# Attention heads by halves: units of half a head, v in two column halves, short runs for o, sums scaled on GpSimd

## The chip, the cores and the metric

One core of a Trainium2 chip runs the whole program. The metric is the device time of one execution in microseconds; the kernel before takes 5920.14 us (median of 3 runs, 5917.19 to 5921.82).

## The reference

The program is four blocks in a row on a tensor of 4 x 96 x 64 x 64: a gated state-space block, a block with window-wise sedenion weights and an MLP, a local attention block with an MLP, and a selective scan. The change lies in the third, whose core is:

```python
qkv = conv1x1(batchnorm(x), qkv_w, qkv_b)            # B=4, 6 heads of 16 channels
qk  = concat([q * scale, k])                          # 32 channels per head
attn = conv7x7(qk, dm_w) + dm_b + rel_bias            # 49 logits per pixel and head
attn = softmax(attn, axis=taps)
out[c, y, x] = sum over 49 taps of v[c, y+dy, x+dx] * attn[tap, y, x]
x1 = x + conv1x1(out, proj_w, proj_b); return x1 + mlp(x1)
```

All is float32. Convolutions run as three TensorE passes over high and low parts (fp32r).

## The kernel before

Three functions matter, each a block of its own with hand-written semaphores.

`attention_qkv` (line 799) projects 32 tiles of 512 pixels. VectorE adds the bias to v and writes it to `v_strip` (line 912), copies the high part of q and k into `strip` (915), GpSimd writes the low part (955), and SP stores both into the padded DRAM scratch `qkv_d` (849, 853; rows of 70). There are two strips, so VectorE waits for the store of two tiles before.

`attention_heads` (963) goes through six heads. A unit is one of 16 channels and one of two rows of a pixel pair. On TensorE a head is 16 convolution chunks of 42 matmuls over 512 pixels (line 1095), evacuated by ScalarE into `logits` (1133); then 16 turns of four transposes (1105) put pixels on the partitions: 128 partitions are 4 images x 32 row pairs, and 64 columns lie in the free dimension. There are three PSUM buffers for turns. VectorE takes the maximum over the taps (1158) and subtracts it (1162), ScalarE exponentiates in four pieces (1138), VectorE sums the totals (1169) and inverts them (1171). Then 32 units follow: a product of 3136 elements (64 columns x 49 taps) of a shifted window of v and attn (1146), on VectorE for 13 units and on GpSimd for 19 (`ON_DVE`), and a sum over the taps on VectorE (1180) for all. GpSimd has two product buffers, VectorE one. `attn` has one buffer, so the softmax of a head comes after all units of the head before; TensorE's convolution of the next head runs beside the units. Last, VectorE scales all sums (1196).

SP's queue, in order: image loads (1033; eight transfers per half image, two buffers, each waiting for the chunks that used the buffer), v loads (1050) that wait for the products of the head before, one store of o (1056).

`attention_out` (1224) loads o, projects it (1297) and runs the MLP. `build` (2138) declares the scratches.

Of the kernel before, what the change touches and what calls it, by code (L numbers as in the profile page):

```python
# [795 lines left out]
STRIP = N // W  # L796


def attention_qkv(nc, w, X, qkv_d, x_d):
# [6 lines left out]
    with ExitStack() as ctx:  # L806
# [10 lines left out]
        zeros = sb("l2a_zeros", [C, 2 * QK + 1, PAD * WP])  # L817
# [3 lines left out]
        v_strip = sb("l2a_v_strip", [C, 2, STRIP, WP])  # L821
# [11 lines left out]
        def _(sp):  # L833
# [5 lines left out]
            for b in range(B):  # L839
                for row in (0, HP - PAD):  # L840
                    sp.dma_start(by_group[:, :, b, row * WP:(row + PAD) * WP], zeros[:]).then_inc(s_pads, 16)
            with sp.Fori(0, B) as b:
                with sp.Fori(0, H // STRIP // 2) as s2:
                    for par in range(2):
                        tile = b * (H // STRIP) + 2 * s2 + par
                        place = bass.ds((PAD + par * STRIP) * WP + s2 * (2 * STRIP * WP), STRIP * WP)
                        sp.wait_ge(s_v, tile + 1)
                        sp.nop(nofuse=True)
                        sp.dma_start(by_group[:, 2 * QK:, bass.ds(b, 1), place],
                                     v_strip[:, par].rearrange("c r x -> c (r x)")).then_inc(s_strip[par], 16)  # L850
                        sp.wait_ge(s_lo, tile + 1)
                        sp.nop(nofuse=True)
                        sp.dma_start(by_group[:, 0:2 * QK, bass.ds(b, 1), place],
                                     strip[:, par].bitcast(F32).rearrange("c p g r x -> c (p g) (r x)")).then_inc(s_strip[par], 16)
            for par in range(2):
                sp.wait_ge(s_strip[par], 32 * (TILES // 2) + STRIP0)
            sp.wait_ge(s_pads, 16 * 2 * B)
# [3 lines left out]
        def _(pe):  # L861
            def qkv(t, par, first=False):
                pe.wait_ge(s_xn, t + 1)
                if not first:
                    pe.wait_ge(s_qk, QK * (t - 1))
                    pe.wait_ge(s_v, t - 1)
# [34 lines left out]
        def _(dve):  # L901
# [7 lines left out]
            def to_strips(t, par):  # L909
                dve.wait_ge(s_mm, t + 1)  # L910
                dve.wait_ge(s_strip[par], 16 * (t - par) + STRIP0)
                dve.tensor_scalar(v_strip[:, par, :, PAD:PAD + W], p_qkv[par][2][:].rearrange("c (r x) -> c r x", x=W),
# [50 lines left out]
def attention_heads(nc, w, qkv_d, o_d):  # L963

# [3 lines left out]
    CHUNKS = PAIRS // CP  # L980
    HB = 2 * B
    HCHUNKS = CHUNKS // 2
    GROWS = 2 * CP * HCHUNKS + SHIFTS - 1
    M = 2 * TAPS
    XT = 4
    TURNS = W // XT
    VC = HD // 2
    UNITS = 2 * HD
    ON_DVE = [u % 5 in (0, 2) for u in range(UNITS)]
    DVE_UNITS = sum(ON_DVE)  # L990
    POOL_UNITS = UNITS - DVE_UNITS
    POOL_PRODS = 2
    EXPS = 4
    with ExitStack() as ctx:
# [10 lines left out]
        logits = sb("l2b_logits", [M, B, PAIRS, W])  # L1005
        attn = sb("l2b_attn", [128, W, 2, TAPS])
        peak = sb("l2b_peak", [128, W, 2])
        total = sb("l2b_total", [128, W, 2])
        v = [sb(f"l2b_v{i}", [128, VC, ROWS, WP]) for i in range(2)]
        prod = [sb(f"l2b_prod{i}", [128, W, TAPS]) for i in range(1 + POOL_PRODS)]  # L1010
        w_full = prod[0][:].rearrange("q x t -> q (x t)")[:, 0:GROUPS * WIN * M]
        osum = sb("l2b_osum", [128, HD, 2, W])
        p_conv = [ps(f"l2b_conv{i}", [M, N]) for i in range(2)]
        p_turn = [ps(f"l2b_turn{i}", [128, XT, 2, TAPS]) for i in range(3)]
        s_w, s_v, s_o = (sem("l2b_" + n) for n in ("weights", "v_loaded", "o_stored"))
        s_img = [sem(f"l2b_img{i}_loaded") for i in range(2)]
        s_bias, s_this, s_conv, s_log, s_turn, s_peak, s_sub, s_exp = (sem("l2b_" + n) for n in (
            "bias", "this_bias", "conv", "logits", "turned", "peak", "shifted", "exp"))
        s_tot, s_rcp, s_pp, s_pv, s_sum, s_osum = (sem("l2b_" + n) for n in (
            "total", "reciprocal", "pool_products", "vector_products", "summed", "scaled"))  # L1020
        block = ctx.enter_context(nc.Block())

        @block.sync
        def _(sp):
            def load_image(head, hb, first=False):

                if not first:
                    sp.wait_ge(s_conv, head * (B * CHUNKS) + (hb - 1) * HCHUNKS)
                    sp.nop(nofuse=True)
                row = hb % 2 * 2 * CP * HCHUNKS  # L1030
                for part in range(2):
                    for s in range(SHIFTS):
                        sp.dma_start(img[part][s * CH:(s + 1) * CH, hb % 2].bitcast(F32).rearrange("c r x -> c (r x)"),
                                     qkv_d[bass.ds(head * CH + part * (2 * C), CH), hb // 2,
                                           (row + s) * WP:(row + s + GROWS) * WP]).then_inc(s_img[hb % 2], 16)

            def load_v(head, first=False):
                for half in range(2):
                    if not first:
                        dve_done = sum(ON_DVE[:(half + 1) * (UNITS // 2)])  # L1040
                        pool_done = (half + 1) * (UNITS // 2) - dve_done
                        sp.wait_ge(s_pv, head * DVE_UNITS + (dve_done - DVE_UNITS))
                        sp.nop(nofuse=True)
                        sp.wait_ge(s_pp, head * POOL_UNITS + (pool_done - POOL_UNITS))
                        sp.nop(nofuse=True)
                    for b in range(B):
                        src = qkv_d[bass.ds(head * HD + (4 * C + half * VC), VC), b]
                        src = bass.AP(src.tensor, src.offset,
                                      [[2 * WP, PAIRS], [B * HP * WP, VC], [1, ROWS * WP]])
                        sp.dma_start(v[half][b * PAIRS:(b + 1) * PAIRS].rearrange("p c r x -> p c (r x)"),  # L1050
                                     src).then_inc(s_v, 16)

            def store_o(head):
                sp.wait_ge(s_osum, head + 1)
                sp.nop(nofuse=True)
                sp.dma_start(o_d[bass.ds(head * HD, HD)].rearrange("c (q z) -> q c z", z=2 * W),
                             osum[:].rearrange("q c r x -> q c (r x)")).then_inc(s_o, 16)

            for dst, src in ((w_full, "w_conv"), (ident[:], "ident"), (dm_b[:], "dm_b"), (rel_b[:], "rel_b")):
                sp.dma_start(dst, w[src].rearrange("c g x m -> c (g x m)") if dst is w_full else w[src]).then_inc(s_w, 16)  # L1060
            load_image(0, 0, first=True)
            load_image(0, 1, first=True)
            load_v(0, first=True)
            for hb in range(2, HB):
                load_image(0, hb)
            load_image(1, 0)
            load_image(1, 1)
            with sp.Fori(1, HEADS - 1) as head:
                for hb in range(2, HB):
                    load_image(head, hb)  # L1070
                load_image(head + 1, 0)
                load_image(head + 1, 1)
                load_v(head)
                store_o(head - 1)
            for hb in range(2, HB):
                load_image(HEADS - 1, hb)
            load_v(HEADS - 1)
            store_o(HEADS - 2)
            store_o(HEADS - 1)
            sp.wait_ge(s_o, 16 * HEADS)  # L1080

        @block.tensor
        def _(pe):
            def conv(head, n, first=False):

                hb, ch = n // HCHUNKS, n % HCHUNKS
                if ch == 0:
                    pe.wait_ge(s_img[hb % 2], 16 * 2 * SHIFTS * (HB // 2) * head + 16 * 2 * SHIFTS * (hb // 2 + 1))
# [1088 lines left out]
```

## Time and profile before

| | us |
|---|---|
| median of 3 runs | 5920.14 |
| the profiled execution | 5919.1 |
| its span | 5917.0 |
| busy: PE, DVE, ACT, POOL | 4968.7, 4826.2, 2914.8, 3855.9 |
| first convolution matmul, last store issued | 1613.82, 2986.03 |

The span runs from the first to the last instruction; the profiled execution's own time holds what lies around it. The last block, the selective scan, takes almost half of the span and is untouched. The page's chain that ended last follows only the end of that block, so for the attention one reads the order of time and the busy times by stretch. TensorE's granted clock is given as a share of its upper level: 1.00 is 2.4 GHz, 0.50 is 1.2 GHz.

### The profile page before, as it was taken

To read this page: it belongs to the slowest core of one execution; us is meant where nothing else is said; L and a number is where in the kernel's file an instruction comes from. 1 tells how busy PE (TensorE), PEld (TensorE's weight loads), DVE (VectorE), ACT (ScalarE), POOL (GpSimd) and SP (SyncE) were. 2 spreads that over 40 slices of the span, in tenths; PEclk is the share of its full clock that TensorE was granted. 3 is DMA by queue.
4 is the path that set the end of the run, shared out by engine and by line. 5 is a ranking of instruction groups with operands and counts; after the bars stand their busy time and mean duration, and the time that the engine had idled before them with its cause. 6 is when DMAs were issued, how large, how long until landed. Compare 5 with 4: busy or idle time off the path is not lost. (4 is left out here: it accounts for less than half of the span.)

```text
span 5917.0 us, 72829 instructions
## 1 busy us (share of the span) xinstructions
PE 4968.7 (84%) x16018; PEld 2212.0 (37%) x16018; DVE 4826.2 (82%) x4793; ACT 2914.8 (49%) x4462; POOL 3855.9 (65%) x2394
## 2 busy tenths in 40 slices
PE   7999899897699889887068888888888888888887
PEld 1222256463266556555034222222222222222222
DVE  4877633434309999999977999999999999999996
ACT  5777534443201000000023777777777776777776
POOL 0000132322307779777966999999999999999993
PEclk9989899998799889888578999999999999999998
DMA  1000000003864655654041667767676777777773
GB/s 45 0 0 0 7 0 1 0 1 114 229 144 103 135 128 123 136 123 106 0 95 28 182 181 191 187 180 191 187 185 186 187 187 188 186 188 186 186 189 101
DMA packets 340815, 707.92 MB, mean 120 GB/s; under 512 B 46717, under 2 KB 63673, under 8 KB 326745
## 3 DMA queue, kind: packets, MB, share of 16 engines
q1 hardware_dynamic: 340568, 705.15, 47.3%
q8 instruction: 92, 1.51, 0.1%
q14 instruction: 155, 1.26, 0.1%
HBM read 572.97 MB, written 81.67 MB: 111 GB/s over the span
## 5 line engine op out<-in xcount | busy, mean ns | idle before, releaser
L1909 POOL TENSOR_TENSOR l_hc<-l_h,l_c_rep 128x512 f32<-128x512 f32 x1536 | 1927.4, 1273 | 210.5 <-DVE l_h L1963 180.1
L1963 DVE TENSOR_TENSOR_SCAN l_h<-l_p_da,l_h,l_bu 128x512 f32<-128x512 f32 x1120 | 1401.7, 1267 | 6.2 <-ACT l_p_da L1814 4.8
L1814 ACT ACTIVATE l_p_da<-l_p_da,l_a_neg 128x512 f32<-128x512 f32 x1536 | 1008.0, 657 | 724.1 <-PE l_p_da L1669 708.5
L1146 POOL TENSOR_TENSOR l2b_prod<-l2b_v,l2b_attn 128x3136 f32<-128x3136 f32 x114 | 990.1, 8700 | 393.0 <-ACT l2b_attn L1138 369.9
L1669 PE MATMUL l_p_da<-l_stacked,l_pick 96*128 96x512 f32 x1536 | 904.0, 590 | 193.6 <-DVE l_h L1963 184.9
L1948 DVE TENSOR_TENSOR l_bu<-l_du_rep,l_p_b 128x512 f32<-128x512 f32 x1280 | 838.5, 655 | 28.5 <-DMA l_du_rep<-du_scratch 22.6
L1669 PEld LDWEIGHTS l_p_da<-l_stacked,l_pick 96*128 96x128 f32 x1536 | 292.9, 191 | 1165.4 <-DVE l_h L1963 908.1
L1180 DVE TENSOR_REDUCE l2b_osum<-l2b_prod 128x64 f32<-128x3136 f32 x192 | 645.9, 3413 | 2.7
L1677 PE MATMUL l_p_y<-l_hc,l_y_pick 128*32 128x512 f32 x3072 | 560.0, 623 | 72.2 <-POOL l_hc L1909 71.5
L1133 ACT ACTIVATE l2b_logits<-l2b_conv,l2b_this_b 98x512 f32<-98x512 f32 x96 | 66.1, 688 | 912.7 <-PE l2b_conv L1095 912.7
L615 POOL TENSOR_TENSOR l_w_pos_low<-l1a_w_sed,l_w_pos_high 96x1536 fp32r<-96x1536 f32 x1 | 4.1, 4126 | 711.5 <-DVE l_w_fc_high L595 711.5
L1146 DVE TENSOR_TENSOR l2b_prod<-l2b_v,l2b_attn 128x3136 f32<-128x3136 f32 x78 | 386.8, 4959 | 2.5
L1095 PE MATMUL l2b_conv<-l2b_img_high,l2b_w_conv_high 128*98 128x512 f32 x1344 | 349.5, 413 | 33.6 <-DMA l2b_img_low<-qkv_scratch 33.6
L1095 PE MATMUL l2b_conv<-l2b_img_high,l2b_w_conv_low 128*98 128x512 f32 x1344 | 338.8, 403 | 0.0
L1095 PE MATMUL l2b_conv<-l2b_img_low,l2b_w_conv_high 128*98 128x512 f32 x1344 | 337.4, 402 | 0.0
L1902 POOL TENSOR_TENSOR l_pool_bu<-l_du_rep,l_b_sb 128x512 f32<-128x512 f32 x256 | 326.2, 1274 | 0.0
L1963 DVE TENSOR_TENSOR_SCAN l_h<-l_p_da,l_h,l_pool_bu 128x512 f32<-128x512 f32 x224 | 284.5, 1270 | 0.8 <-ACT l_p_da L1814 0.7
L1095 PEld LDWEIGHTS l2b_conv<-l2b_img_high,l2b_w_conv_high 128*98 128x98 f32 x1344 | 226.7, 169 | 140.5 <-issue 31.7
L770 POOL TENSOR_TENSOR l1b_h_h_low<-l1b_h_h,l1b_h_h_high 128x512 fp32r<-128x512 f32 x96 | 125.5, 1319 | 226.8 <-DVE l1b_h_h_high L734 226.8
L1095 PEld LDWEIGHTS l2b_conv<-l2b_img_high,l2b_w_conv_low 128*98 128x98 f32 x1344 | 219.8, 164 | 103.6
L1095 PEld LDWEIGHTS l2b_conv<-l2b_img_low,l2b_w_conv_high 128*98 128x98 f32 x1344 | 219.8, 164 | 102.1
L1297 PE MATMUL l2c_p_x<-l2c_o,l2c_w_proj 96*96 (+1 forms) x64 | 34.6, 626 | 209.7 <-DMA x_back<-x_scratch 209.7
(265 smaller groups left out, 8964.7 us busy)
## 6 DMA issues: line engine op xcount, KB each, us to landing
l_du_rep<-du_scratch SPq DMA_DIRECT2D x1536, 256.0 KB, 3.9
l2b_img_high<-qkv_scratch SPq DMA_DIRECT2D x192, 306.2 KB, 5.5
l2b_img_low<-qkv_scratch SPq DMA_DIRECT2D x192, 306.2 KB, 9.2
l_stacked<-l_parts SPq DMA_DIRECT2D x512, 96.0 KB, 2.7
qkv_scratch<-l2a_strip SPq DMA_DIRECT2D x32, 840.0 KB, 5.1
l2b_v<-qkv_scratch SPq DMA_DIRECT2D x48, 560.0 KB, 16.9
du_scratch<-l_du SPq DMA_DIRECT2D x128, 192.0 KB, 2.2
qkv_scratch<-l2a_v_strip SPq DMA_DIRECT2D x32, 210.0 KB, 4.0
```

Of the source, the lines that this page charges most:

```text
L770: pool.tensor_tensor(h_hl[1][:, f, :], h[:, f, :], h_hl[0][:, f, :], ALU.subtract).then_inc(s_h_lo, 1)
L1095: mm = pe.matmul(p_conv[n % 2][:], w_conv[w_part][:, g, dx, :], img[x_part][:, hb % 2, row:row + 2 * CP - 1:2, dx:dx + W], start=(at == 0) ...
L1133: act.activation(logits[:, b, CP * ch:CP * (ch + 1), :].rearrange("m p x -> m (p x)"), p_conv[n % 2][:], ACT.Identity, bias=this_b[:]).the ...
L1146: return eng.tensor_tensor(dst.rearrange("q x (dy dx) -> q x dy dx", dx=WIN), window, attn[:, :, r].rearrange("q x (dy dx) -> q x dy dx", ...
L1180: dve.tensor_reduce(osum[:, unit // 2, unit % 2, :], prod[which][:], AX_X, ALU.add).then_inc(s_sum, 1)
L1669: pe.matmul(p_da[i % DAS][:], pick[:, GRP[i] % (Q // DL), :], stacked[:, par, GRP[i] * DL // Q, :], start=True, stop=True).then_inc(s_rep, 1)
L1677: mm = pe.matmul(p_y[par][q * 32:(q + 1) * 32, :], y_pick[:, t, :], hc[:, (G * par + YT * t + q) % HCS, :], start=(t == 0), stop=False)
L1814: act.activation(p_da[i % DAS][:], p_da[i % DAS][:], ACT.Exp, scale=a_neg[:, k * G + GRP[i]:k * G + GRP[i] + 1]).then_inc(s_da, 1)
L1902: pool.tensor_tensor(pool_bu[:, at, :], du_rep[:, ring_at(par, i)], b_sb[:], ALU.mult).then_inc(s_pbu, 1)
L1909: pool.tensor_tensor(hc[:, (G * par + i) % HCS, :], h[:, i, :], c_rep[:, par, :], ALU.mult).then_inc(s_hc, 1)
L1948: dve.tensor_tensor(bu[:, i % BUS, :], du_rep[:, ring_at(par, i)], p_b[par][:], ALU.mult).then_inc(s_bu, 1)
L1963: dve.tensor_tensor_scan(h[:, i, way], p_da[i % DAS][:, way], of, state, ALU.mult, ALU.add).then_inc(s_h, 1)
```

## The change

- A job is half a head: 16 row pairs of each image, twelve jobs. The partitions are 2 column halves x 4 images x 16 row pairs, the free dimension has 32 columns. Products and totals have 1568 elements, a job has 8 chunks, 8 turns and 32 units (9 on VectorE, 23 on GpSimd).
- `attn`, `total` and `osum` have two halves. The softmax of job j+1 stands inside the units of job j (`SOFTMAX_AT`, `TOTALS_AT`).
- ScalarE copies v for VectorE's nine units into three PSUM banks; VectorE's products read v from there. VectorE has two product buffers, GpSimd four.
- GpSimd scales the sums of job j-1 after its second product of job j.
- v has a DRAM scratch of its own, `v_d`: two column halves of 38 columns each that overlap in six. It is loaded in runs of 1216 B (2240 B before) in 8 transfers per 8 channels, and `attention_qkv` writes it with two VectorE instructions per tile. Two transfers zero its pad rows; the eight for q and k get four groups instead of five.
- o is stored per job in 8 transfers of 256 runs of 256 B (before, per head, one of 2048 runs of 512 B). `attention_out` reads it with a strided matmul operand.
- SP's order per job: images 2 and 3 of the next job, the first half of v, images 0 and 1 of the job after, the second half of v, the store of o.

```diff
-    POOL_PRODS = 2
-    EXPS = 4
+    JOBS = HALVES * HEADS
+    DVE_UNITS = 9
+    ON_DVE = [u * DVE_UNITS % UNITS < DVE_UNITS for u in range(UNITS)]
+    POOL_PRODS = 4
+    DVE_PRODS = 2
+    PV_BANK = (0, 1, 2, 0, 1, 2, 0, 1, 2)
+    EXPS = 2
+    SOFTMAX_AT = 26
+    TOTALS_AT = 29
+    SCALE_AT = 2
+    COPY_AFTER = {1: (3,), 2: (4,), 3: (5,), 4: (6,), 5: (7,), 6: (8,)}
...
             def store_o(j, head, half):
                 sp.wait_ge(s_osum, j + 1)
+                for xh in range(XH):
+                    for b in range(B):
...
+                        sp.dma_start(dst, osum[at:at + HP_PAIRS, half].rearrange("q c r x -> q c (r x)")).then_inc(s_o, 16)
...
+            def job(j, head, half, has_next, has_second):          # SP
+                if has_next:
+                    load_image(j + 1, *following(head, half), 2)
+                    load_image(j + 1, *following(head, half), 3)
+                    load_v(j + 1, *following(head, half), 0)
+                if has_second:
+                    load_image(j + 2, head + 1, half, 0)
+                    load_image(j + 2, head + 1, half, 1)
+                if has_next:
+                    load_v(j + 1, *following(head, half), 1)
+                store_o(j, head, half)
...
+            def copy_v(j, at, first):                              # ScalarE
+                act.wait_ge(s_v[c // VC], 16 * XH * B * j + 16 * XH * B)
+                before = used_before(PV_BANK, at)
+                if not first or before >= 0:
+                    act.wait_ge(s_pv, j * DVE_UNITS + before + 1)
+                act.activation(p_v[PV_BANK[at]][:], v[c // VC][:, c % VC, r:r + WIN, 0:VX], ACT.Copy).then_inc(s_vcp, 1)
+            def job(j, head, half, has_next, has_second):
+                copy_v(j, 0, first)
+                if has_next:
+                    bias(j + 1, nhead)
+                    evacuate(j + 1, nhalf, 0)
+                copy_v(j, 1, first)
+                copy_v(j, 2, first)
+                for n in range(1, JCHUNKS):
+                    if has_next:
+                        evacuate(j + 1, nhalf, n)
+                    for at in COPY_AFTER.get(n, ()):
+                        copy_v(j, at, first)
+                if has_next:
+                    exps(j + 1, nhalf)
...
+            def own_product(j, half, unit):                        # VectorE
+                dve.wait_ge(s_vcp, j * DVE_UNITS + at + 1)
...
+                products(dve, windows(p_v[PV_BANK[at]][:], VX), attn[:, half], unit, prod[at % DVE_PRODS][:]).then_inc(s_pv, 1)
+            def job(j, head, half, has_next, has_second):
+                dve.wait_ge(s_o, 16 * STORES * j + 16 * STORES)
                 for unit in range(UNITS):
+                    if unit == SOFTMAX_AT and has_next:
+                        softmax(j + 1, 1 - half)
+                    if unit == TOTALS_AT and has_next:
+                        totals(j + 1, 1 - half)
                     if ON_DVE[unit]:
+                        own_product(j, half, unit)
+                    sums(j, half, unit)
-                dve.tensor_tensor(osum[:], osum[:], inverse, ALU.mult).then_inc(s_osum, 1)
...
+            def scale(j, half):                                    # GpSimd
+                pool.wait_ge(s_sum, j * UNITS + UNITS)
+                pool.wait_ge(s_rcp, j + 1)
+                pool.tensor_tensor(osum[:, half], osum[:, half], inverse, ALU.mult).then_inc(s_osum, 1)
```

## Rows read from the trace of the kernel before

**Rows 1.** The page, costliest groups (busy and mean us/ns, then idle before)

```profile
L1146 POOL TENSOR_TENSOR l2b_prod<-l2b_v,l2b_attn 128x3136 f32<-128x3136 f32 x114 | 990.1, 8700 | 393.0 <-ACT l2b_attn L1138 369.9
```

**Rows 2.** Busy us by stretch (start:end, length, engines, granted clock, DMA)

```profile
1984.00:2004.00 20.00, 16.67 (x65) 11.78 (x66) 19.45 (x35) 6.26 (x5) 0.35 (x1) 0.53 0.86 183
...
2004.00:2184.00 180.00, 160.47 (x673) 109.48 (x671) 178.98 (x50) 11.02 (x16) 165.11 (x19) 0.95 0.56 122
```

**Rows 3.** The order of time, second head, units (start, us, engine, line)

```profile
2020.45 3.43 DVE L1146 TENSOR_TENSOR l2b_prod<-l2b_v,l2b_attn 128x3136 f32<-128x3136 f32 x1
...
2020.49 9.93 POOL L1146 TENSOR_TENSOR l2b_prod<-l2b_v,l2b_attn 128x3136 f32<-128x3136 f32 x1 [0.29 <-DVE l2b_osum L1180]
...
2034.01 6.68 DVE L1146 TENSOR_TENSOR l2b_prod<-l2b_v,l2b_attn 128x3136 f32<-128x3136 f32 x1
...
2047.55 9.97 POOL L1146 TENSOR_TENSOR l2b_prod<-l2b_v,l2b_attn 128x3136 f32<-128x3136 f32 x1 [0.30 <-DVE l2b_osum L1180]
```

**Rows 4.** Instructions that write or read attn (ns min/median/max)

```profile
L1146 POOL TENSOR_TENSOR l2b_prod<-l2b_v,l2b_attn x114: 6529/9855/9994, 1803.3 to 2966.9; 128x3136 f32<-128x3136 f32 x114
```

**Rows 5.** The order of time, end of convolution and softmax

```profile
1782.84 0.69 ACT L1133 ACTIVATE l2b_logits<-l2b_conv,l2b_this_b 98x512 f32<-98x512 f32 x1 [9.34 <-PE l2b_conv L1095]
...
1783.57 1.84 PEld L1105 LDWEIGHTS l2b_turn<-l2b_ident,l2b_logits 98*128 98x128 f32 x12 [1.24 <-ACT l2b_logits L1133]
...
1785.05 0.57 DVE L1162 TENSOR_TENSOR l2b_attn<-l2b_turn,l2b_peak 128x392 f32<-128x392 f32 x1
...
1789.96 0.66 PEld L1105 LDWEIGHTS l2b_turn<-l2b_ident,l2b_logits 98*128 98x128 f32 x4 [0.41 <-DVE l2b_attn L1162]
...
1793.16 1.55 ACT L1138 ACTIVATE l2b_attn<-l2b_attn 128x1568 f32<-128x1568 f32 x1 [2.75 <-DVE l2b_attn L1162]
...
2001.84 6.86 DVE L1169 TENSOR_REDUCE l2b_total<-l2b_attn 128x32 f32<-128x1568 f32 x4
```

**Rows 6.** The order of time, chunks of the third head after a softmax

```profile
1999.40 4.65 PEld L1095 LDWEIGHTS l2b_conv<-l2b_img_high,l2b_w_conv_high 128*98 128x98 f32 x14
...
2011.30 0.69 ACT L1133 ACTIVATE l2b_logits<-l2b_conv,l2b_this_b 98x512 f32<-98x512 f32 x1 [7.74 <-PE l2b_conv L1095]
...
2162.50 0.69 ACT L1133 ACTIVATE l2b_logits<-l2b_conv,l2b_this_b 98x512 f32<-98x512 f32 x1 [9.34 <-PE l2b_conv L1095]
```

**Rows 7.** SP's issues of one image, and us from issue to landing (img_low)

```profile
2021.66 1.86 SPq L1033 DMA_DIRECT2D l2b_img_high<-qkv_scratch  x4
...
2023.73 1.96 SPq L1033 DMA_DIRECT2D l2b_img_low<-qkv_scratch  x4
...
DMA to landing us min/median/max: 7.3/9.2/19.9
```

**Rows 8.** Transfers in 2986:2992 (the last store) and 1984:1988 (v loads)

```profile
q1 hardware_dynamic: 2064, 1.05, 61.5%
...
o_scratch<-l2b_osum SPq DMA_DIRECT2D x1, 1024.0 KB, 5.1
...
DMA packets 386, 0.82 MB, mean 206 GB/s; under 512 B 18, under 2 KB 18, under 8 KB 386
```

**Rows 9.** Products and differences by source line (ns min/median/max)

```profile
L1909 POOL TENSOR_TENSOR l_hc<-l_h,l_c_rep x1536: 1250/1272/1304, 3254.7 to 5829.1; 128x512 f32<-128x512 f32 x192
...
L1948 DVE TENSOR_TENSOR l_bu<-l_du_rep,l_p_b x1280: 648/654/689, 3243.0 to 5824.7; 128x512 f32<-128x512 f32 x183
...
L955 POOL TENSOR_TENSOR l2a_strip<-l2a_qk,l2a_strip x32: 2165/2342/2449, 1446.4 to 1588.1; 96x1024 fp32r<-96x1024 f32 x32
```

**Rows 10.** The order of time, first and last of the heads, and one scaling

```profile
1613.82 4.58 PEld L1095 LDWEIGHTS l2b_conv<-l2b_img_high,l2b_w_conv_high 128*98 128x98 f32 x14 [31.73 <-issue]
...
1982.45 2.29 DVE L1196 TENSOR_TENSOR l2b_osum<-l2b_osum,l2b_total 128x2048 f32<-128x2048 f32 x1
...
2986.03 0.41 SPq L1056 DMA_DIRECT2D o_scratch<-l2b_osum  x1
```

**Rows 11.** The order of time, one tile of the projection stage

```profile
1500.14 0.75 DVE L912 TENSOR_SCALAR l2a_v_strip<-l2a_p,l2a_bias 96x512 f32<-96x512 f32 x1 [3.41 <-DMA qkv_scratch<-l2a_strip]
```

More of the change, by code:

```diff
@@ L1021, in attention_heads, with all_jobs, following, used_before @@
         block = ctx.enter_context(nc.Block())
+        def all_jobs(job, eng):
+            job(0, 0, 0, True, True)
+            with eng.Fori(0, HEADS - 2) as i:
+                job(2 * i + 1, i, 1, True, True)
+                job(2 * i + 2, i + 1, 0, True, True)
+            for j in range(JOBS - 3, JOBS):
+                job(j, j // 2, j % 2, j + 1 < JOBS, j + 2 < JOBS)
+        def following(head, half):
+            return (head, 1) if half == 0 else (head + 1, 0)
+        def used_before(buffers, at):
+            n = len(buffers)
+            return max(a for a in range(at - n, at) if buffers[a % n] == buffers[at])
@@ L1061, in _ @@
[L1061 to L1080, printed above, removed]
+                        sp.dma_start(img[part][s * CH:(s + 1) * CH, b % 2].bitcast(F32).rearrange("c r x -> c (r x)"),
+                                     qkv_d[bass.ds(head * CH + part * (2 * C), CH), b,
+                                           (row + s) * WP:(row + s + GROWS) * WP]).then_inc(s_img[b % 2], 16)
@@ L1208, in _ @@
+            softmax(0, 0)
+            totals(0, 0)
+            all_jobs(job, dve)
         @block.gpsimd
         def _(pool):
[L1210 to L1217 removed]
@@ new lines, in job @@
+            def job(j, head, half, has_next, has_second):
+                first = isinstance(j, int) and j == 0
+                pool.wait_ge(s_exp, j * EXPS + EXPS)
+                mine = [unit for unit in range(UNITS) if not ON_DVE[unit]]
+                for at, unit in enumerate(mine):
+                    c, r = unit // 2, unit % 2
+                    if at == SCALE_AT and not first:
+                        scale(j - 1, 1 - half)
+                    if at == 0 or c // VC != mine[at - 1] // 2 // VC:
+                        pool.wait_ge(s_v[c // VC], 16 * XH * B * j + 16 * XH * B)
+                    before = used_before([a % POOL_PRODS for a in range(POOL_UNITS)], at)
+                    if before >= 0:
+                        pool.wait_ge(s_sum, j * UNITS + (mine[before] + 1))
+                    elif not first:
+                        pool.wait_ge(s_sum, j * UNITS + (mine[before] + 1 - UNITS))
+                    window = windows(v[c // VC][:, c % VC, r:r + WIN, 0:XW], VX)
+                    products(pool, window, attn[:, half], unit, prod[DVE_PRODS + at % POOL_PRODS][:]).then_inc(s_pp, 1)
@@ L1319, in _, with step @@
         def _(act):
[L1320 removed]
+            def step(t, q, project, mlp_in, mlp_out, load, image):
                 if mlp_in:
```

332 lines of the change are left out of this document (180 added, 152 removed).

## The prediction

> **What bounds the kernel now.** I read the page's groups first, then the busy time by stretch, then the order of time inside one head. The change lies in the attention heads, between the first convolution matmul at 1613.82 and the last store, issued at 2986.03 and landed 5.1 us later, at 2991.1 [rows 10, 8]: 1377.3 us. In them GpSimd's products are the costliest group [rows 1]. In a stretch of 180 us inside a head VectorE is busy 178.98, GpSimd 165.11, TensorE 160.47 us; in the 20 us of softmax at its start GpSimd does almost nothing (0.35), and TensorE's clock is low (0.53) [rows 2]. The two stretches repeat every 200 us, once a head.
>
> The order of time shows that VectorE's 178.98 is not all work [rows 3]. A VectorE product takes 3.43 us when it begins just before GpSimd's; GpSimd's product, begun 0.04 us later, then takes 9.93, against 6.53 at its shortest [rows 4]: 6.5 + 3.4. The next time GpSimd is first, and VectorE's product takes 6.68. So the products of both, each with two SBUF inputs, exclude each other. A group of five units has 3 x 6.53 + 2 x 3.43 = 26.5 us in this one place, and it recurs after 27.1 (GpSimd's long products begin at 2020.49 and 2047.55). The heads are therefore bound by that exclusion for 32 units, and by softmax in series. TensorE has room, little of it.
>
> **The change, part by part.**
>
> *Products.* VectorE takes v from a copy in PSUM, made by ScalarE, so it has one SBUF input. The trace of the attention does not show such a product beside GpSimd's. The nearest row is in the last stage: 1280 VectorE multiplications of one SBUF and one PSUM input (648 to 689 ns) beside GpSimd's 1536, which all stay between 1250 and 1304 ns [rows 9]. Nothing there grows by another's length, so I take the exclusion as gone. Bounds: none of it gone, or all.
>
> *GpSimd per half head* (a "job", twelve of them). 23 products of 1568 elements. Half of 6.53 is 3.26; 1024 elements take 2.17 at least, which gives 3.32 in proportion; 512 take 1.27, in proportion 3.9 [rows 4, 9]. The first two are nearest in size: 3.33. Scaling the sums, moved here from VectorE, is 1024 elements: 2.17 to 2.45 [rows 9], I take 2.25. Sum: 23 x 3.33 + 2.25 = 78.8 us.
>
> *VectorE per job.* 32 sums of 1568 elements to 32: four such follow each other in 6.86 us [rows 5], 1.71 each, 54.7. Nine products: 392 elements with one PSUM input take 0.57, of which 392/3136 x 3.27 = 0.41 is streaming (3.27 being 3.43 less about the same 0.16), so 1568 take 1.63 + 0.16, and 0.03 until the sum may follow: 1.82, 16.4 in all. At the least it is half of 3.43 (1.71); at the most PSUM is read at half speed (3.5). Softmax: 8 pairs of maximum and subtraction. The first subtraction starts at 1785.05; the exponential that waits for the eighth starts at 1793.16, so the eighth starts 0.6 before: 7.5 over seven, 1.075 each [rows 5], 8.6. Totals 3.4, and an estimate of 0.6 for the reciprocal of 64. Sum: 83.7 us. The scaling (2.29 us a head [rows 10]) leaves VectorE.
>
> *TensorE per job.* 8 chunks at the pace of ScalarE's evacuations: fifteen from 2011.30 to 2162.50, 10.08 us each [rows 6]: 80.6. From the end of the last chunk over its evacuation to the first turn 0.95 (the evacuation starts at 1782.84, 0.2 after the matmuls; the turn at 1783.57). Turns 0 to 7: from 1783.57 to 1789.96 + 0.66 = 1790.62, 7.05 us, because turn 7 needs VectorE's subtraction of turn 4 [rows 5]. Then the clock: in softmax it is granted at 0.53 [rows 2], and the chunk after it runs from 1999.40 to 2011.30, 11.9 us against 10.08 [rows 6]: 1.8. The new gap is 8 us, not 36, so the loss may be less; bounds 0 and 1.8, I take 1.8, the row. Sum: 80.6 + 0.95 + 7.05 + 1.8 = 90.4 us (88.6 without the clock's part). That is longer than VectorE's 83.7 and GpSimd's 78.8: **TensorE becomes the bound.**
>
> *Do the three fit together?* Let t = 0 be the end of turn 7. Turn 7 ended at 1790.62, so VectorE's last subtraction ends at 2.5 and the exponential (1793.16 + 1.55) at 4.1 [rows 5]. Units 26 to 28 of the old job are summed by 7.5, totals by 11.5, product 29 by 13.3, sums 29 to 31 by 18.5. Unit 26 of the new job is then reached 26 x 1.71 + 8 x 1.82 = 59 us later, near 77.6 and with waits for GpSimd's products some 4 us more; turn 0 is there at 84.1. GpSimd does its first new product from 7.5 (its buffer is free after sum 28), its second only after sum 30, at 16.7, then scales: done 22.4. The other 21 take 69.9: 92.3, of which four buffers are ahead of VectorE. So both stay within 90.4, VectorE by about 3 us and GpSimd by about 5. Softmax in series is gone, and what is late next is the convolution.
>
> *SP's queue.* The store of a job waits for the scaling (22.4) and stands in front of the next image's load, which could otherwise go at 22, when chunks 0 and 1 are done. Eight stores take 8 x 0.41 us to issue [rows 10]: the image is issued from 25.7. Its eight transfers take, on a free queue, from 2021.66 to the last issue's end at 2025.69 and about 8.5 more, 12.4 us in all [rows 7]; that is 38.1. TensorE needs it at 42.1. Before it in the queue lie 2048 packets of 256 B. Before, 2048 packets of 512 B took 61.5% of 16 engines for 6 us, 29 ns of an engine each [rows 8]. At equal time per byte they take 1.8 us, at equal time per packet 3.7, and with twice that, 7.4. The stores begin with the first issue, so the image's data begin at 27 or, at worst of these, 31: it lands at 39 to 43. I take 0 wait; the cover is about 3 us, and beyond it each us costs one per job. The v loads (1024 packets of 1216 B per half; 386 packets were 0.82 MB in 4 us, 166 ns of an engine per 2240 B [rows 8], so 6.1 us by bytes, 10.6 by packets) go in at 13.3 and are through by 20 to 24: within cover.
> The Trainium skill ("DMA: Bandwidth & Descriptors", Specifications) gives 512 B as the least transfer at line rate and says that shorter ones are a read-modify-write. No row shows such a store. If that doubles a packet's time, it is the 7.4 us above, 0.5 us per cycle, and the sum would be 5 us higher.
>
> *ScalarE* gains 9 copies of 266 elements per job. 512 take 0.69 [rows 5], so at most that, 6 us in 90: hidden between evacuations 10 us apart. A copy that waits for a product holds up the evacuations queued behind it, and through them TensorE; the tightest is the third, which waits for product 29 (13.3) in front of the evacuation due at 22: 8 us of cover.
>
> *Around the heads.* In the projection stage VectorE's write of v, 0.75 us after a wait for the store of two tiles before [rows 11], becomes two of 280 elements, about 0.5 each. 16 round trips of two tiles each gain 0.25, and 1.7% more bytes: +4 us (0 to 8). Pads, the read of o, and the matmul's strided operand: same bytes, hidden behind loads: 0.
>
> **The sum.** From the first matmul: job 0's chunks, the first at low clock, 11.9 + 7 x 10.08 = 82.5; gap and turns 8.0; 11 cycles of 90.4 = 994.4; the last job's products and scaling 96.3 after its turn 7 (92.3, sum 1.7, scaling 2.3); seven issues and the last one's 5.1 to landing, 8.0. Together 1189.2, against 1377.3: -188. With +4: 5917.0 - 184 = 5733 span. The profiled execution is 5919.1, 2.1 above its span, and 1.0 under the median of 5920.1: **5736**.
>
> **Rivals.**
> 1. *The exclusion stays* (the copy in PSUM frees nothing). GpSimd's place holds 78.8 + 9 x 1.82 = 95.2, plus part of the wait for sum 30: 99 us per cycle, +8.6 x 11, and +13 in the last job: 5843. For it: nothing in a row of the attention. Against: rows 9.
> 2. *The image comes late.* Small packets cost over 60 ns, or the scaling ends later. With 5 us per cycle: 5791. For it: a cover of 3 us. Against: 29 ns per packet.
> 3. *The vector engines bind*, at 1.9 to 2.0 us a sum, 3.6 to 3.9 a GpSimd product or a slow PSUM read: cycles of 92 to 99, 5753 to 5836. For it: small margins, windows of 7 elements never read from PSUM before.
> 4. *No clock loss:* cycle 88.6, 5714. For it: the gap is shorter.
> 5. *Slower: the clock.* Everything now hangs on TensorE at its upper level (2.4 GHz; granted 1.0). If low stretches (0.5, 1.2 GHz) spread from the turns into the chunks, a cycle of 107.5 equals before: chunks of 98 instead of 80.6, a mean grant near 0.83. All at 0.5: 80 us more per job, near 6690. For it: every softmax pulls the clock down [rows 2]. Against: it recovers within the first chunk, and 180 us of chunks keep 0.95 [rows 2].
>
> **How the numbers follow.** Forecast 0.58; late image 0.12; exclusion 0.07; vector engines 0.13; no clock loss 0.07; slower by the clock 0.03. The forecast's own spread (5 us clock and stage, 0 to 2 us per cycle of unseen waits) is 5720 to 5765. The 8-in-10 range takes in the no-loss case and most of the late image and of rival 3: 5707 to 5808. A change under 0.2% (12 us) can't be told from none: 0.01. Slower 0.03, faster 0.96.
>
> **What would show it.** GpSimd's products near 3.3 us without long ones beside VectorE's; VectorE's near 1.8; turn groups 90 us apart; VectorE waiting for the turns a few us per job, TensorE with no wait for an image; each first chunk near 11.9. The forecast is wrong if TensorE waits for VectorE's subtraction at turn 3 in each job by more than 1 us, or for an image, or if GpSimd's products come in two lengths.

## The result, and the profile after

The changed kernel takes 5746.01 us (median of 4 runs, 5743.74 to 5751.83) against 5920.69 us before (4 runs, 5917.19 to 5921.82): ratio 0.9707, interval 0.9691 to 0.9724. The prediction was 5736, in a range of 5707 to 5808. The profiled execution after takes 5744.95 us, its span 5743.1, so the two profiled spans differ by 173.9.

All of it comes from the attention heads, the part that computes the logits, the softmax and the weighted sums. From the first convolution matmul to the next block's first load, before took 2992.4 - 1613.8 = 1378.6 us; after it is 2810.93 - 1616.3 = 1194.6, or 184.0 less. Their first matmul comes 2.5 us later: the projection stage got 5.3 us longer (from its first matmul at 1439.3 to 1613.8 before, from 1436.5 to 1616.3 after), and the unchanged code ahead of it was 2.8 us shorter in this execution. What follows the heads took 7.6 us more, in code that is the same but for the read of o.

The heads themselves changed in two places. The fill, from the first matmul to the first turn, went from 169.8 to 83.6 us (-86.1). The rest, from there to the issue of the last store (after: of the first of its eight transfers, at 2803.99), went from 1202.5 to 1104.0 (-98.5).

The page after: the busy line, and the two groups that answer to [rows 1]:

```profile
PE 4971.3 (87%) x16018; PEld 2207.8 (38%) x16018; DVE 4640.4 (81%) x5047; ACT 2949.7 (51%) x4576; POOL 3832.2 (67%) x2568
...
L1221 POOL TENSOR_TENSOR l2b_prod<-l2b_v,l2b_attn 128x1568 f32<-128x1568 f32 x276 | 937.3, 3461 | 242.9 <-DVE l2b_osum L1269 125.2
...
L1269 DVE TENSOR_REDUCE l2b_osum<-l2b_prod 128x32 f32<-128x1568 f32 x384 | 665.7, 1780 | 62.9 <-POOL l2b_prod L1221 59.2
```

GpSimd's 276 products of half the size take 937.3 us, its 114 of before took 990.1. The instructions around attn (minimum, median, maximum in ns) answer to [rows 4]:

```profile
L1221 POOL TENSOR_TENSOR l2b_prod<-l2b_v,l2b_attn x276: 3349/3452/3626, 1711.0 to 2796.0; 128x1568 f32<-128x1568 f32 x138
L1221 DVE TENSOR_TENSOR l2b_prod<-l2b_p_v,l2b_attn x108: 1727/1781/1793, 1713.2 to 2794.5; 128x1568 f32<-128x1568 f32 x108
```

No product has two lengths any more. Before, GpSimd's median was 9855 against a minimum of 6529; now the largest is 8% over the least. One cycle by stretch, as in [rows 2]: TensorE's share is now the highest.

```profile
1984.00:2184.00 200.00, 192.32 (x809) 131.43 (x808) 184.18 (x132) 25.00 (x45) 173.68 (x53) 0.97 0.76 138
```

TensorE's cycle in the order of time, from the evacuation of a job's last chunk over the eight turns to the evacuation of the next job's first chunk:

```profile
1969.48 0.69 ACT L1174 ACTIVATE l2b_logits<-l2b_conv,l2b_this_b 98x512 f32<-98x512 f32 x1 [9.05 <-PE l2b_conv L1139]
...
1970.22 1.58 PE L1149 MATMUL l2b_turn<-l2b_ident,l2b_logits 98*128 98x98 f32 x12 [0.78 <-ACT l2b_logits L1174]
...
1976.47 0.92 PE L1149 MATMUL l2b_turn<-l2b_ident,l2b_logits 98*128 98x98 f32 x4 [0.16 <-DVE l2b_attn L1238]
...
1988.40 0.69 ACT L1174 ACTIVATE l2b_logits<-l2b_conv,l2b_this_b 98x512 f32<-98x512 f32 x1 [6.81 <-PE l2b_conv L1139]
```

The turns take 7.17 us (1970.22 to 1977.39). The first chunk takes 11.0 us from there, against 10.1 for a chunk at full clock; over the eleven cycles it is 10.8 to 12.2, 11.4 on average. The granted clock (the third number from the right) is at its lower level (0.50, 1.2 GHz) in the turns and back at the upper (1.00) in the stretch from 1980, 3 us after the chunk's start at 1977.09:

```profile
1974.00:1976.00 2.00, 1.69 (x10) 1.23 (x8) 1.93 (x5) 0.63 (x1) 2.00 (x2) 0.50 1.00 206
1976.00:1978.00 2.00, 1.84 (x8) 1.29 (x8) 1.93 (x5) 0.89 (x1) 1.61 (x1) 0.50 1.04 230
1978.00:1980.00 2.00, 2.00 (x7) 1.34 (x6) 1.97 (x4) 0.33 (x1) 0.00 (x0) 0.69 1.00 221
1980.00:1982.00 2.00, 2.00 (x10) 1.36 (x9) 2.00 (x2) 1.59 (x3) 0.60 (x1) 1.00 0.82 166
```

The waits between 1790 and 2790 us (total, times, longest):

```profile
POOL l2b_prod L1221 <- DVE l2b_osum L1269: 125.2, 22, 15.1
...
DVE l2b_peak L1234 <- PE l2b_turn L1149: 36.8, 11, 12.8
...
PE l2b_conv L1139 <- DMA l2b_img_low<-qkv_scratch: 7.9, 4, 2.8
```

VectorE waits 36.8 / 11 = 3.3 us a job for the turns and GpSimd has slack. TensorE waits four times for an image, which the prediction had at nothing. The first turns of the twelve jobs start at 1699.95, 1789.69, 1880.19, 1970.22, ..., 2699.93: eleven cycles of 90.91 on average.

The image waits cost more than they last, most of it in one of them. In the order of time, SP's issues: the last store of a job, image 2 of the next, and then image 3:

```profile
2003.86 0.32 SPq L1097 DMA_DIRECT2D o_scratch<-l2b_osum  x1
2007.49 1.87 SPq L1067 DMA_DIRECT2D l2b_img_high<-qkv_scratch  x4
2009.57 1.81 SPq L1067 DMA_DIRECT2D l2b_img_low<-qkv_scratch  x4
2018.81 1.81 SPq L1067 DMA_DIRECT2D l2b_img_high<-qkv_scratch  x4
```

Between the store and the image lie 3.3 us in which nothing is issued. This recurs twice (2186 to 2189.3, 2368.8 to 2372.2), where SP's loop, which holds two jobs and runs four times, goes from one iteration to the next; elsewhere the gap is 0.1 to 0.5. In each of the three gaps two packets of the queue that loads instructions move; this is the DMA view of 2004.2 to 2007.5:

```profile
q14 instruction: 2, 0.02, 1.2%
```

In the ordinary gap near 2096.5 there are none. So I put the 3.3 us down to the loop's branch back and the loading of its instructions; no run takes it apart. The image is then late. Two of the waits that follow, the longest and the dearest:

```profile
2021.34 1.92 PE L1139 MATMUL l2b_conv<-l2b_img_high,l2b_w_conv_high 128*98 128x512 f32 x7 [2.76 <-DMA l2b_img_low<-qkv_scratch]
```

```profile
2386.12 6.27 PE L1139 MATMUL l2b_conv<-l2b_img_high,l2b_w_conv_high 128*98 128x512 f32 x14 [2.65 <-DMA l2b_img_low<-qkv_scratch]
...
2392.21 3.56 PE L1139 MATMUL l2b_conv<-l2b_img_high,l2b_w_conv_low 128*98 128x512 f32 x14
...
2399.17 0.69 ACT L1174 ACTIVATE l2b_logits<-l2b_conv,l2b_this_b 98x512 f32<-98x512 f32 x1 [14.69 <-PE l2b_conv L1139]
```

Their stretches of 2 us:

```profile
2020.00:2022.00 2.00, 0.66 (x3) 0.51 (x4) 2.00 (x2) 0.00 (x0) 2.00 (x2) 1.00 1.05 240
2022.00:2024.00 2.00, 2.00 (x10) 1.37 (x9) 1.97 (x3) 0.00 (x0) 2.00 (x2) 1.00 1.02 221
...
2386.00:2388.00 2.00, 1.88 (x5) 1.32 (x6) 2.00 (x2) 0.00 (x0) 2.00 (x1) 0.50 1.05 221
...
2390.00:2392.00 2.00, 2.00 (x6) 1.36 (x5) 2.00 (x3) 0.00 (x0) 2.00 (x2) 0.50 0.98 216
2392.00:2394.00 2.00, 2.00 (x9) 1.32 (x9) 1.59 (x1) 0.00 (x0) 2.00 (x1) 0.94 0.98 211
```

After the wait of 2.65 us at 2386 the granted clock is 0.50 for six microseconds. Fourteen matmuls take 6.27 us instead of 3.56, and the chunk's evacuation comes 15.7 after the one before (2383.51), not 10.1. After the wait of 2.76 us at 2021 the clock stays at 1.00, and the evacuation comes 13.1 after the one before. The four waits (1.0, 2.8, 1.6 and 2.7 us) add 7.9 us by themselves and 11.6 by the evacuations (gaps of 11.3, 13.1, 11.9 and 15.7), so 2.9 of the 3.7 us between the two belong to the one wait after which the clock fell. The first wait, of 1.0 us at 1838.85, comes in a job without the gap of 3.3 us: there the image was issued 0.5 us after the stores, at 1823.60, and TensorE got it 15.2 us later.

The last store, as in [rows 8] (stretch of 8 us):

```profile
q1 hardware_dynamic: 2176, 0.52, 38.7%
...
o_scratch<-l2b_osum SPq DMA_DIRECT2D x8, 64.0 KB, 2.3
```

That is 0.387 x 8 x 16 / 2176 = 23 ns of an engine for a packet of 256 B, against 29 for 512 B.

### The profile page after: what moved, and what is told of

Its sections match the earlier page's. It is cut to its first block and busy times, and to the rows that moved or that the text cites. A ratio compares the mean times of both kernels' runs of the same rounds, so it can differ in the third digit from the quotient of the medians.

```text
span 5743.1 us, 74310 instructions
## 1 busy us (share of the span) xinstructions
PE 4971.3 (87%) x16018; PEld 2207.8 (38%) x16018; DVE 4640.4 (81%) x5047; ACT 2949.7 (51%) x4576; POOL 3832.2 (67%) x2568
## 3 DMA queue, kind: packets, MB, share of 16 engines
q8 instruction: 100, 1.64, 0.1%
## 5 line engine op out<-in xcount | busy, mean ns | idle before, releaser
L1221 POOL TENSOR_TENSOR l2b_prod<-l2b_v,l2b_attn 128x1568 f32<-128x1568 f32 x276 | 937.3, 3461 | 242.9 <-DVE l2b_osum L1269 125.2
L2054 DVE TENSOR_TENSOR l_bu<-l_du_rep,l_p_b 128x512 f32<-128x512 f32 x1280 | 855.7, 669 | 29.7 <-DMA l_du_rep<-du_scratch 22.5
L1269 DVE TENSOR_REDUCE l2b_osum<-l2b_prod 128x32 f32<-128x1568 f32 x384 | 665.7, 1780 | 62.9 <-POOL l2b_prod L1221 59.2
L1759 PE MATMUL l_p_bc<-l_relu_x,l_ident 96*96 96x512 f32 x256 | 144.6, 648 | 66.5 <-ACT l_c_rep L1916 59.3
L2069 DVE TENSOR_TENSOR_SCAN l_h<-l_p_da,l_bu 128x512 f32<-128x512 f32 x160 | 192.6, 1222 | 7.7 <-ACT l_p_da L1920 7.6
```

The source lines that it names most:

```text
L1221: return eng.tensor_tensor(dst.rearrange("q x (dy dx) -> q x dy dx", dx=WIN), window, attn_half[:, :, unit % 2].rearrange("q x (dy dx) -> ...
L1269: dve.tensor_reduce(osum[:, half, unit // 2, unit % 2, :], prod[which][:], AX_X, ALU.add).then_inc(s_sum, 1)
L1759: pe.matmul(p_bc[0:C, :], ident[:], relu_x[:], start=True, stop=False)
L2054: dve.tensor_tensor(bu[:, i % BUS, :], du_rep[:, ring_at(par, i)], p_b[par][:], ALU.mult).then_inc(s_bu, 1)
L2069: dve.tensor_tensor_scan(h[:, i, way], p_da[i % DAS][:, way], of, state, ALU.mult, ALU.add).then_inc(s_h, 1)
```

## Experiments

Each is the changed kernel with one edit (or the two or three named); lines of a diff that are left out are marked with dots. Besides the median I compare the heads alone, in the profiled execution: from the first convolution matmul to the next block's first load. The rest, the same code in all ten kernels but for a few lines, varies by more than the smaller effects: the first matmul starts between 1613.8 and 1632.8, and what follows the heads takes 2923.2 to 2937.8. The cycles of e1 to e8 are the mean of the ten from the second job's softmax to the last's, that of after is the mean of all eleven (its ten are 91.0). The ratios are to runs of the kernel before that were made beside each batch: median 5922.66 for e1 to e4, 5927.35 for e5 to e8.

| kernel | median us | ratio to before, interval | heads us | cycle us |
|---|---|---|---|---|
| before | 5920.69 | | 1378.6 | 100.2 (half of 200.4) |
| after | 5746.01 | 0.9707, 0.9691 to 0.9724 | 1194.6 | 90.9 |
| e1 v from SBUF | 5856.76 | 0.9891, 0.9876 to 0.9906 | 1305.1 | 100.7 |
| e2 two passes | 5677.30 | 0.9594, 0.9575 to 0.9614 | 1131.0 | 88.2 |
| e3 image first | 5735.41 | 0.9689, 0.9676 to 0.9703 | 1183.9 | 89.9 |
| e4 serial softmax | 5757.02 | 0.9734, 0.9715 to 0.9754 | 1204.0 | 92.9 |
| e5 e3, chunk between turns | 5721.71 | 0.9663, 0.9644 to 0.9681 | 1165.9 | 88.5 |
| e6 e5, totals later | 5700.96 | 0.9626, 0.9607 to 0.9645 | 1148.6 | 86.9 |
| e7 e3, totals later | 5748.39 | 0.9696, 0.9681 to 0.9711 | 1182.6 | 89.9 |
| e8 e1 and e4 | 5927.86 | 1.0002, 0.9987 to 1.0017 | 1369.3 | 106.6 |

### e1: VectorE reads v from SBUF

Is the exclusion of the two engines' products really what the copy in PSUM removes?

```diff
-                products(dve, windows(p_v[PV_BANK[at]][:], VX), attn[:, half], unit, prod[at % DVE_PRODS][:]).then_inc(s_pv, 1)
+                products(dve, windows(v[c // VC][:, c % VC, r:r + WIN, 0:XW], VX), attn[:, half], unit, prod[at % DVE_PRODS][:]).then_inc(s_pv, 1)
...
```

> The changed kernel, but VectorE reads v from SBUF again and ScalarE's copies are gone; nothing else differs. Theory (products with two SBUF inputs on VectorE exclude GpSimd's): GpSimd's products come in two lengths, 3.4 and about 5.1 us, VectorE's in 1.8 and up to 5 us; GpSimd's place holds 23 x 3.4 + 2.4 + 9 x 1.8 = 97 us of a job plus some 4 us of waiting for buffers, so a cycle of 99 to 101 us instead of 90.9, and 13 us more in the last job: 5746 + 8 to 10 x 11 + 13 = 5847 to 5870. Rival (the gain came from the order by halves alone, TensorE hides the rest): VectorE and GpSimd had 3 to 5 us of room in a cycle, so at most 5750 to 5765.

Measured: 5856.76 and a cycle of 100.7, both as expected; heads +110.5 us. The products:

```profile
L1222 POOL TENSOR_TENSOR l2b_prod<-l2b_v,l2b_attn x276: 3352/3444/5073, 1712.7 to 2906.5; 128x1568 f32<-128x1568 f32 x138
L1222 DVE TENSOR_TENSOR l2b_prod<-l2b_v,l2b_attn x108: 1727/3270/3448, 1714.9 to 2905.0; 128x1568 f32<-128x1568 f32 x108
```

VectorE's median is 3270, its minimum still 1727: it does not stream more slowly, it stands and waits for GpSimd's product to end. The order of time has it:

```profile
1986.76 3.37 POOL L1222 TENSOR_TENSOR l2b_prod<-l2b_v,l2b_attn 128x1568 f32<-128x1568 f32 x1
...
1988.67 3.10 DVE L1222 TENSOR_TENSOR l2b_prod<-l2b_v,l2b_attn 128x1568 f32<-128x1568 f32 x1
1990.08 4.94 POOL L1222 TENSOR_TENSOR l2b_prod<-l2b_v,l2b_attn 128x1568 f32<-128x1568 f32 x1
```

GpSimd's product ends at 1990.13, VectorE's 1.64 us later, and GpSimd's next takes 1.6 us longer than alone. Of VectorE's 108 products 97 begin inside one of GpSimd's, and all 97 end 1.64 to 1.66 us after it; the other 11 take 1.73. GpSimd's longest, 5073, is close to 3350 + 1727. Both lengths are about those of before, halved. The Trainium skill ("SBUF — State Buffer", Who interferes with whom) says that a VectorE instruction with two SBUF inputs contends with a GpSimd instruction that reads SBUF and that one with a single SBUF input, outside the two-port modes, doesn't. These two kernels agree, at 110.5 us for 108 products.

### e2: two convolution passes instead of three

Is TensorE the bound, and how far below it do the vector engines lie? The edit shortens TensorE's chunks by a third.

```diff
-                passes = [(w_part, x_part, g, dx) for w_part, x_part in ((0, 0), (1, 0), (0, 1))
+                passes = [(w_part, x_part, g, dx) for w_part, x_part in ((0, 0), (1, 0))
```

> The changed kernel, but the convolution of the attention heads makes two of its three passes (the low part of q and k is left out), so a chunk is 28 matmuls instead of 42, 6.7 us instead of 10.1. Theory (TensorE sets the cycle, the vector engines follow 2 to 3 us behind): the first job's chunks save 27 us, and the cycle falls from 90.9 to where VectorE and GpSimd end, 87.5 to 88.7, 24 to 37 us in eleven cycles: 5682 to 5695; VectorE no longer waits for turns. Rival 1 (the vector engines are the bound already): only the 27 us, 5719. Rival 2 (TensorE alone, the others have much room): cycle near 64, 5746 - 27 x 12 = 5422.

Measured: 5677.3, 5 us below the expected 5682 to 5695. The cycle is where it was expected, at a second bound just below the first: it goes from 90.9 to 88.2 only, though TensorE lost 27 us of work in it. TensorE now waits for VectorE's subtractions and for images:

```profile
PE l2b_conv L1139 <- DMA l2b_img_low<-qkv_scratch: 133.6, 10, 16.1
...
PE l2b_turn L1149 <- DVE l2b_attn L1238: 101.6, 49, 11.2
...
POOL l2b_prod L1221 <- DVE l2b_osum L1269: 86.6, 21, 5.7
```

The GpSimd row closes the sum. Its 23 products at 937.3 / 276 = 3.40 us and a scaling of 2.44 are 80.6; with 86.6 / 11 = 7.9 of waiting for VectorE in each job that is 88.5. So the two vector engines together need 88.2 in this order of their units, TensorE 89.9 without image waits (e3) and 90.9 with them. The rest of the 63.6 us that the heads lose is in the fill (60.6 us to the first turn, not 83.6) and in the first cycle, which is 13 us shorter; the expectation had not counted that one apart.

### e3: the image ahead of the store

```diff
                 if has_next:
                     load_image(j + 1, *following(head, half), 2)
+                if not (isinstance(j, int) and j == 0):
+                    store_o(j - 1, *(((head, 0) if half else (head - 1, 1))))
...
-                store_o(j, head, half)
...
+            store_o(JOBS - 1, HEADS - 1, 1)
```

> The changed kernel, but SP issues the load of the next job's image 2 before the store of o, not after it. In the trace of the change the evacuations of chunk 3 and chunk 4 are over 10.1 us apart in four of eleven cycles (11.3, 13.1, 11.9, 15.7: 11.6 us too long in all), where TensorE waited for that image. Theory (the store and the jump of SP's loop in front of it make it late, and the wait then costs the clock too): all eleven are 10.1, TensorE waits for no image after the first job: 5746 - 11 = 5735. Rival (the image is late by its own transfer or by the v loads in front of it): the waits stay, 5746; if the store now hinders the load of image 3: longer.

Measured: 5735.41; heads -10.7 us, cycle 89.86, and no wait of TensorE for an image after the first job. The eleven cycles together are 11.6 us shorter, as much as the evacuations had shown, so that is what the queue's order cost. The edit takes the stores and the gap of 3.3 us out from in front of the image together and doesn't say how much of it is either's. The interval of the ratio overlaps that of the change, so for the size I rely on the heads.

### e4: the softmax behind the units

```diff
-                    if unit == SOFTMAX_AT and has_next:
-                        softmax(j + 1, 1 - half)
-                    if unit == TOTALS_AT and has_next:
...
-                        totals(j + 1, 1 - half)
...
+                if has_next:
+                    softmax(j + 1, 1 - half)
...
+                    totals(j + 1, 1 - half)
```

> The changed kernel, but the softmax and the totals of the next job stand behind all 32 units of a job, not among them. VectorE's work is the same. Theory (the overlap matters because GpSimd works during the softmax): GpSimd idles in the softmax and in the exponential, 8.6 + 1.5 us, then needs 23 x 3.4 + 2.4 = 80.6, and VectorE 1.7 more: a cycle of 93 to 96 us instead of 90.9, 5769 to 5802. Rival (only the exclusion mattered, VectorE's sum of work is unchanged and TensorE is the bound): 5746 within 5 us.

Measured: 5757.02, below what I expected. GpSimd now waits for the exponential, as it did before the change:

```profile
POOL l2b_prod L1221 <- ACT l2b_attn L1182: 134.9, 11, 12.3
```

That is 12.3 us a job, and 80.6 + 12.3 = 92.9 is the cycle, just under the 93 to 96 that I expected. What I had not counted is the end: from the last job's first turn to the issue of the last store it is 97.3 us, not 104.1, since no unit of the job before stands behind the last softmax. The eleven cycles from first turn to first turn add 16.7 us, the end takes 6.8 off and the fill 0.5, which makes the heads 9.4 longer. The overlap alone is worth 2.0 us a cycle by the table, so little because TensorE bounds the changed kernel, where GpSimd already waited 125.2 us for VectorE; and at 92.9 no image is late.

### e5: part of the first chunk between the turns

In the turns TensorE waits for VectorE and its clock falls. e5 is e3 with ten of the next job's convolution matmuls put ahead of turns 3 to 7.

```diff
+                    if has_next and 2 <= g < 7:
+                        conv(j + 1, 0, lo=AFTER * (g - 2), hi=AFTER * (g - 1))
...
```

> The kernel with the image ahead of the store (5735.4, cycle 89.86), in which TensorE also makes two matmuls of the next job's first chunk after each of turns 2 to 6, ten in all, while it would wait for VectorE. Theory (TensorE sets the cycle, and the turns cost it 7 us of waiting and a low clock): ten matmuls are 2.4 us, and if the clock no longer falls up to 1.8 more, so TensorE alone would need 85.7 to 87.5; VectorE and GpSimd end at 88.2, the cycle seen with two passes, so 88.2: 5735 - 1.6 x 11 = 5717. Rival 1 (the turns are delayed, and VectorE waits): 5735 or more. Rival 2 (the vector engines don't follow behind TensorE at 88.2 when the images are late less often): 5709 to 5690.

Measured: 5721.71; heads 18.0 less than e3's. TensorE's cycle by stretches of 2 us, in the turns of the fourth job:

```profile
1974.00:1976.00 2.00, 2.00 (x9) 1.56 (x9) 1.93 (x5) 0.00 (x0) 2.00 (x1) 0.50 0.97 206
1976.00:1978.00 2.00, 2.00 (x13) 1.63 (x12) 1.97 (x4) 1.42 (x1) 2.00 (x2) 0.77 1.04 221
1978.00:1980.00 2.00, 2.00 (x12) 1.55 (x12) 1.93 (x5) 0.10 (x1) 2.00 (x1) 1.00 1.06 235
```

In these rows TensorE is busy throughout. It still waited once for VectorE, 1.70 us at 1973.39, and the clock still fell; but the upper level is back by 1978, while turns go on until 1979, and in the changed kernel it was back by 1980. The cycle is 88.5, which is where e2 put the vector engines.

### e6 and e7: the totals two units later

If the vector engines bind e5, then moving VectorE's totals from unit 29 to 31, so that GpSimd's buffers come free earlier, must help there, and must not help where TensorE binds. e6 is e5 with it, e7 is e3 with it.

```diff
-    TOTALS_AT = 29
+    TOTALS_AT = 31
```

> As the kernel with interleaved turns, and the totals of the next job stand before unit 31 instead of before unit 29. Sums 29 and 30 then come 4 us sooner, and with them GpSimd's free buffers, for whose want it idles 5.7 us a job. Theory (the vector engines' end of the cycle is set by that idle time of GpSimd): their 88.2 falls to about 86.7, and the cycle to 86.7 to 87.5, the larger of the two: 5700 to 5709. Rival (VectorE's own work is the floor, its waits for GpSimd aside): 5717 as without the move.

> The kernel with the image ahead of the store, and of the two later edits only the move of the totals before unit 31. Theory (TensorE sets the cycle at 89.86, GpSimd's idle time costs nothing there): 5735, within 4 us (the last job's start gains 2). Rival (GpSimd and VectorE are the bound, or share it): 1.5 us less per cycle, 5719.

Measured: e6 5700.96, at the lower end of what was expected, heads another 17.3 less, cycle 86.9; e7's heads are 1.3 less than e3's and its cycle is the same 89.9. GpSimd's waits for VectorE fall in both, but only e6 has a use for it:

```profile
POOL l2b_prod L1231 <- DVE l2b_osum L1279: 52.8, 22, 11.3
```

(e6; 96.3 in e5.) In e7 the same row goes from e3's 113.6 to 87.1. e7's median of 5748.39 stands 13 above e3's and outside the 4 us I had allowed. Its profile puts that ahead of the heads: the second block's weights are issued at 720.7, 13.3 later than in e3 (707.4), in code that is the same in both. Between 200 and 400 us the granted clock was 0.90 there, 0.95 in e3. Why it differs is open.

### e8: e1 and e4 together

What is left of the change with neither the PSUM copy nor the overlap? The half-head unit, the split of 9 and 23 units, and the scaling on GpSimd stay in.

> The changed kernel with both undone: VectorE reads v from SBUF, and the softmax stands behind the units. What is left of the change is half a head as unit of work, the split of units, and the moved scaling. Theory (half a job's convolution in front of everything instead of a whole one is worth 170 - 84 = 86 us, and the exclusion and the series of softmax take it back): GpSimd's place 23 x 3.4 + 9 x 1.8 + 3 = 97 us, softmax and exponential 10, last sum 2: a cycle of 105 to 109 against 90.9, 5746 + 11 x 14 to 18 + 16 = 5916 to 5960. Rival (the effects overlap: once the exclusion binds, serial softmax costs nothing more): 5857, as with v from SBUF alone.

Measured: 5927.86 (10 runs, 5913.7 to 5951.88), ratio 1.0002, within what was expected. The heads are 9.3 us shorter than before, in a cycle of 106.6:

```profile
PE l2b_turn L1149 <- DVE l2b_attn L1239: 189.9, 55, 17.5
...
POOL l2b_prod L1222 <- ACT l2b_attn L1182: 135.2, 11, 12.4
```

The same wait of GpSimd for the exponential in the kernel before, for the last five heads (1850 to 3000):

```profile
POOL l2b_prod L1146 <- ACT l2b_attn L1138: 156.8, 5, 31.4
```

The fill's 86 us are there (the first turn comes 83.8 us after the first matmul), but each half head costs 6.4 us more than before, twelve times: +77. The series of softmaxes isn't the reason, for GpSimd waits 12.3 us at each of eleven here and waited 31.4 at each of five before, which is 3.4 less per half head. The rest of the cycle grew by 9.8 us, from 84.5 to 94.3. By the lengths at their shortest, (19 x 6.53 + 13 x 3.43) / 2 = 84.3 us of products stood in this one place before. The new split adds 4 x (3.35 - 1.73) = 6.5, the scaling on GpSimd 2.4, and products of half the size 1.8, together 10.7. So most of the loss, by this estimate, belongs to a split of units that pays only without the exclusion, and to the scaling; no run has the half-head unit with the old split. From here the PSUM copy alone (e4) takes 165.3 us off the heads, the overlap alone (e1) 64.2, and both together 174.7, not 229.5: with both, TensorE bounds the cycle.

## Why the prediction was right

- **Exclusion gone.** Right. One length of product on each engine, and e1 brings back the two lengths and 110.5 us. The largest single step.
- **TensorE becomes the bound, at 90.4 a cycle.** Right in kind: the measured mean is 90.91, or 89.85 without the image waits. The terms: chunks 10.05 against 10.08, turns 7.17 against 7.05, the clock's part 0.9 in the cycle shown and 1.3 on average (0.8 to 2.1) against 1.8. Taking the row of before for a gap a quarter as long was too much. e2 shows the margin to the vector engines as 1.7 to 2.7 us, where the prediction had 3 for VectorE and 5 for GpSimd, since GpSimd's 23 products and VectorE's softmax make each other wait.
- **The image: 0 wait from a cover of 3 us.** Wrong by 11.6 us, the largest error inside the heads, and one of the three signs that the prediction named against itself (TensorE waits for an image). The packets are not the reason: 23 ns each is less than the 29 taken from [rows 8], and none took the doubled time. The stores began where they should (22.6 us after turn 7, predicted 22.4). Three terms of the cover failed. The image's issue came at 26.8, not 25.7, and in the three jobs after a loop's branch at 30.1. From the issue to TensorE's next matmul it took 13.7 to 15.2 us, not the 12.4 read from [rows 7]; before, that same image took 13.4 to land. And TensorE was ready for it at 41.0 to 42.3, not 42.1, since the clock mostly took less. So the cover was under 2 us even without the branch's 3.3, and in one job it was gone without it. Rival 2 had the place right, at a fifth of its price, and for another reason.
- **What cancelled.** Without the images the eleven cycles would be 6.0 us under the sum, mostly by the clock's part; the images add 11.6. That the cycles came out only 5.6 over it is luck in part.
- **Durations.** GpSimd's product 3.40 to 3.45, against 3.33; its scaling 2.44, against 2.25; VectorE's product 1.78 against 1.79, its sum 1.73 to 1.78 against 1.71. Off by up to 8%, and hidden, since neither engine binds.
- **First and last job.** Fill to the first turn 83.6, predicted 83.45. From the last job's first turn to the first of the last stores 104.1, predicted 7.05 + 96.3 = 103.35. The stores, up to the next block's first load, 6.9 us against 9.3, as a transfer lands after 2.3 us and not 5.1.
- **Projection stage.** +5.3, predicted +4 (0 to 8). The write of v is two instructions of 0.50 and 0.51 us, as taken. The code ahead of it, unchanged, was 2.8 us shorter.
- **Slips in the sums.** The v load by bytes is 5.8 us, not 6.1, and a cycle of 99 gives 5831 in rival 3, not 5836. Nothing hung on either.
- **The sum.** Heads predicted 1190.5 on the scale used here (1189.2 to the landing, and 1.3 from there to the next load, as before), measured 1194.6: cycles +5.6, last job +0.7, fill +0.2, stores -2.4. Ahead of the heads it is -1.5 (+1.3 for the projection stage, -2.8 for the code before it). From the last projection matmul of `attention_out` to the end it is +7.4 (2730.8 us against 2723.4 before). Together that is the 10 us between 5733 and 5743.1. The code of that last part is untouched, and e2 took 2721.9 for it, e4 2722.8 and e1 2732.8, so this part is variation and not the change.

## What to carry to other kernels

Half the unit pays in the fill, 86 us here, and lets the serial part of one unit run beside the work of the other. What it costs in the loop by itself no run shows; the split of work between two engines should be chosen for the kernel in which it stands, as 9 and 23 units cost an estimated 6.5 us a job where the engines exclude each other. Add up the waits, not only the work, for the second-busiest engine: with 80.6 us of work in a cycle of 90 GpSimd still bound from 88 on. Once TensorE is the bound, each of its waits is paid in full, and one in four was paid a second time by the clock. So a cover of 3 us in a DMA queue should be counted as none, and loads that TensorE needs go ahead of stores that nobody waits for. The version of e6 takes 5700.96 us and beats both kernels.

## What the runs showed of the hardware

- While VectorE reads two inputs from SBUF and GpSimd does too, one waits for the other: in e1 97 of VectorE's 108 products begin inside one of GpSimd's, and all end 1.64 to 1.66 us after it. With v in PSUM no product of GpSimd takes over 3.63 us, against 5.07.
- Between two iterations of SP's loop 3.3 us pass without an issue (three times in the trace of after), and two packets of instructions are loaded in each; between the two jobs inside one it is 0.3.
- TensorE's granted clock stayed at 0.50 for six microseconds after a wait of 2.65 us, which cost 5.6 us in all. After one of 2.76 us it stayed at 1.00, and the cost was 3.0. The length of the wait alone doesn't tell.
- A store of 256 B runs takes 23 ns of a DMA engine per packet, of 512 B runs 29: the shorter costs 1.6 times as much per byte.
- GpSimd's scaling of 1024 elements takes 2371 to 2446 ns beside VectorE's instructions with one SBUF input. In e1, where the products have two, eleven of twelve take 3.94 to 4.01 us.
